# Weight maxima spread over TensorE, and experts' weights loaded in seven parts around tiles in the projections' place

## The chip, the cores and the metric

The kernel runs on one core of a Trainium2 chip. Its time is in microseconds (us) of device time, from the start of the program to its last instruction. A core has TensorE (PE, with its weight loads PEld), VectorE (DVE), ScalarE (ACT), GpSimd (POOL) and SyncE (SP, which here only issues transfers); 16 DMA engines move data. Each engine runs its own instructions in order and waits on semaphores for the others. A wait holds back all that stands behind it on that engine, transfers that it would issue included.

## The reference, cut to what matters

```python
xn = layernorm(x)                                  # x: 4 x 1024 x 512
q, k, v = heads(xn @ Wq.T + bq), ...               # 16 heads of 32
s = q @ k.T / sqrt(32), causal, minus slope * distance
attn = softmax(s) @ v                              # then @ Wo.T + bo
probs = softmax(xn @ gate_w.T)                     # 4096 tokens, 8 experts
topw, sel = top_k(probs, 2); topw /= topw.sum()
g, u = split(xn @ w1[e].T)                         # 2 x 352
ffn = sum over the two chosen e of topw * (silu(g) * u) @ w2[e].T
out = x + attn + ffn
```

All is float32. The kernel writes each operand of a projection as a float16 number and a float16 remainder ("high" and "low"), and forms three of the four products. For that each weight matrix is scaled by a power of two that comes from its largest absolute value.

## The kernel before, in words

`plan()` writes one list of steps. Each engine walks this list and emits its own instructions in that order, so a step's place in the list is its place in every queue it touches. `sync`, `tensor`, `vector`, `scalar` and `gpsimd` hold the instructions of each step. `Once` leaves out waits that are already covered.

**Opening.** SP loads eight tiles of x (128 tokens each), then `bcol`, the gate's weights, four chunks of Wq/Wk/Wv (`w0` to `w3`, 128x1536 each), Wo and the constants `cF`. ACT's queue loads `bv` and `bo` at the very start. A tile is normalized (`bn`, `rsq`, `newton` on POOL, `xn`), split (`xnh` on ACT, `xnl` on POOL), turned on TensorE (`xtp`) and copied out (`xt`). Then come the maxima: `tops` takes each partition's largest value of four chunks on DVE, `gtops` takes the largest over the partitions on POOL (`partition_all_reduce`), `scales` makes the factors, and `wqh` (ACT) and `wql` (DVE) make high and low of each of the four chunks. The projections of batch 0, head group 0 (`qkv_steps(0, 0)`) follow: four `qk` groups of 12 matmuls, each handed on by `qk32` (ACT), `qkh` (DVE) and `qkl` (POOL), and two `v` groups of 48. Woven between them stand `otop`, `gotop`, `woh`, `wol` (the same for Wo), `gwh`, `gwl` and the gate's matmuls of batch 0. `stack` then moves q and k by DMA to where the scores read them.

**Attention.** 512 units (batch, head group, row block, head): `score` on TensorE, `mx` (DVE, adds the distance term and takes the maximum), `exp` (ACT), `tr` (TensorE), `pt` (a copy on ACT or DVE, whichever has less to do), and per 8 units `pv` and `rt`. Later projections, the experts' weight split (`wmax`, `wsh`, `wsl`, `wstore`) and the routing are jobs that give a few steps per unit. The output projection `o` has 12 matmuls for each of 8 row blocks of a batch, `y` (DVE) adds x, `ostore` stores it. The routing leaves the token lists in `tl` (`listr`).

**Experts.** 71 slots of 128 tokens: `gather` (POOL, indirect DMA), `mxt` (DMA transpose, issued by SP), `mgu` (24 matmuls), `msig`, `mglu`, `mah`, `mal` (ACT and DVE), `mat` and `mac` (turned again), `mdn` (9 matmuls, seven slots behind at first), `myo`, and `scatter` (POOL, adds to the output). All weights of the experts lie in SBUF in that phase: 32 pieces, 16 of w1 (704 KB) and 16 of w2 (384 KB). `win` loads them into words 0 to 34816 of `arena` as room comes free there: `win(0)` in place of the projections' weights and of the turned x, `win(1)` in place of the group buffers, `win(2)` (one piece of w1, all of w2) in place of what the last units use. The experts' own tiles (`xg`, `xT`, `ex`, `ac`, `ah`, `aTm`) lie behind the weights and begin after the last unit.

## Time and profile before

| | us |
|---|---|
| median of three runs (1664.79 to 1666.81) | 1664.9 |
| the profiled execution | 1675.45 |
| its span | 1673.6 |
| first `mx` of the attention begins | 83.8 |
| last `o` matmul ends | 1211.3 |
| first `mgu` begins | 1234.0 |
| first `mdn` begins | 1269.0 |

A row of a timeline gives start and length in us, engine, source line, operation, what it writes and reads, how many were merged (x), and in brackets how long the engine had been idle before it and what released it. "issue" stands for a time in which the profile shows no releaser. Mean TensorE clock over the span was 0.96 of full speed.

### The profile page before, as it was taken

What the parts mean: (1) busy time and instruction counts of PE and PEld (TensorE: products, weight loads), DVE (VectorE), ACT (ScalarE), POOL (GpSimd) and SP (SyncE); (2) the same over time, 40 slices, a digit from 0 to 9 for tenths busy, and PEclk for the clock granted to TensorE, in tenths of its full rate; (3) what the DMA queues carried; (4) which work ended last, traced back from release to release, by engine and by line L of the source; (5) the groups of instructions that cost most, each with busy time, mean ns of one, the idle gap of its engine ahead of it and who ended that gap; (6) DMA issues with size and microseconds to landing.
All of it is one profiled execution on the core that took longest, in us unless ns stands there. A gap on an engine that the chain in (4) does not pass through costs nothing.

```text
span 1673.6 us, 35255 instructions
## 1 busy us (share of the span) xinstructions
PE 1473.7 (88%) x12629; PEld 879.6 (53%) x12629; DVE 1027.9 (61%) x2452; ACT 887.7 (53%) x2027; POOL 605.6 (36%) x647
## 2 busy tenths in 40 slices
PE   1599998998998899989799888799949999999995
PEld 1355555555555555655455444455436656565563
DVE  5488778665778767777878846568414333333331
ACT  3277667665777666676766446568312222222221
POOL 3111132121113312112311355351214677777775
PEclk9899999999999999999999889799979999999998
DMA  6053431243243253542214233154286888888884
GB/s 246 18 133 110 133 106 60 72 127 105 92 135 89 74 143 115 151 125 80 91 61 119 83 100 83 49 166 177 93 252 107 133 135 129 131 142 138 129 139 51
DMA packets 173685, 193.42 MB, mean 116 GB/s; under 512 B 89616, under 2 KB 123408, under 8 KB 173392
## 3 DMA queue, kind: packets, MB, share of 16 engines
q1 hardware_dynamic: 143760, 151.22, 33.4%
q0 software_dynamic: 28176, 37.31, 13.5%
q8 instruction: 109, 1.79, 0.4%
q10 hardware_dynamic: 1584, 2.64, 0.4%
q14 instruction: 56, 0.46, 0.1%
HBM read 93.45 MB, written 53.88 MB: 88 GB/s over the span
## 4 chain that ended last, share of the span: by engine, by line
PE 65%; DVE 11%; issue 9%; ACT 5%; SPq 4%; DMA 4%; POOL 2%; another core or an unknown queue 2%; DVEq 0%; ACTq 0%; POOLq 0%
PE S L1074 15%; PE T L1006 11%; PE O L1022 7%; PE S L995 5%; PE M L963 5%; PE S L963 4%; PE O L1105 4%; PE M L1105 4%; SPq L855 3%; DVE arena L1361 3%; PE M L1045 2%; ACT arena L1533 2%; PE S L980 2%; DVE arena L1372 1%
## 5 line engine op out<-in xcount | busy, mean ns | idle before, releaser
L1361 DVE CUSTOM_DVE_ANT_0 arena<-S,cF,nsl 128x1024 f32<-128x1024 f32 (+7 forms) x512 | 413.7, 812 | 69.9 <-PE S L995 60.4
L1006 PE MATMUL T<-cF,arena 128*128 128x128 f32 x2304 | 373.3, 283 | 87.7 <-ACT arena L1543 46.7
L1533 ACT ACTIVATE arena<-arena,mneg 128x1024 f32<-128x1024 f32 (+7 forms) x512 | 395.3, 772 | 44.6 <-DVE mneg L1361 44.1
L1543 ACT ACTIVATE arena<-T 128x512 f32<-128x512 f32 (+3 forms) x543 | 242.2, 459 | 290.2 <-PE T L1006 258.9
L1006 PEld LDWEIGHTS T<-cF,arena 128*128 128x128 f32 x2304 | 270.6, 143 | 193.5 <-issue 53.2
L1074 PE MATMUL S<-arena 128*128 x1704 | 267.7, 314 | 23.0 <-issue 23.0
L1696 POOL DMA_INDIRECT out<-arena,row x142 | 222.3, 1566 | 104.0 <-ACT arena L1595 42.1
L1372 DVE COPY arena<-T 128x512 f32<-128x512 f32 (+3 forms) x289 | 154.0, 535 | 151.5 <-PE T L1006 135.5
L1074 PEld LDWEIGHTS S<-arena 128*128 128x128 f16 x1704 | 167.0, 98 | 120.4 <-issue 23.6
L1022 PE MATMUL O<-arena 128*32 128x128 f32 (+1 forms) x3328 | 214.2, 334 | 8.1 <-DVE arena L1392 6.8
L995 PE MATMUL S<-arena 96*128 96x512 f16 (+3 forms) x768 | 216.1, 336 | 5.5 <-DVE mneg L1361 3.0
L1640 POOL TENSOR_TENSOR arena<-arena 128x512 f16<-128x512 f32 x64 | 74.3, 1161 | 277.1 <-DVE arena L1342 270.0
L1468 DVE COPY arena<-T 128x512 f16<-128x512 f16 x71 | 30.2, 425 | 210.8 <-PE T L1089 186.5
L1650 POOL CAST arena<-arena 128x256 f16<-128x256 f32 x64 | 26.5, 414 | 342.6 <-DVE arena L1392 342.4
L1022 PEld LDWEIGHTS O<-arena 128*32 128x32 f32 x3328 | 67.6, 109 | 132.3 <-issue 116.6
L1580 ACT ACTIVATE arena<-S,sc 128x352 f32<-128x352 f32 x71 | 39.3, 554 | 179.5 <-PE S L1074 166.0
L963 PE MATMUL M<-arena 128*128 128x512 f16 x384 | 99.6, 388 | 14.9 <-DVE arena L1286 14.9
L1657 POOL TENSOR_TENSOR arena<-arena 128x512 f32<-128x512 f32 x32 | 41.0, 1291 | 163.3 <-DMA arena<-in_x 163.3
L1533 ACT ACTIVATION_READ_ACCUMULATOR arena<-arena,mneg 128x1 f32 x512 | 99.9, 195 | 0.0
L963 PE MATMUL S<-arena 128*128 128x512 f16 x384 | 99.8, 388 | 0.0
L1683 POOL DMA_INDIRECT arena<-xn_d,tl x71 | 72.8, 1025 | 60.3 <-DMA arena<-arena 39.3
L1588 ACT ACTIVATE arena<-arena 128x352 f16<-128x352 f32 x71 | 35.2, 496 | 110.4 <-DVE arena L1454 99.5
(169 smaller groups left out, 1808.3 us busy)
## 6 DMA issues: line engine op xcount, KB each, us to landing
arena<-arena SPq DMA_DIRECT2D x192, 128.0 KB
arena<-in_w1T SPq DMA_DIRECT2D x64, 352.0 KB
arena<-in_x SPq DMA_DIRECT2D x64, 256.0 KB, 3.3
w_d<-arena SPq DMA_DIRECT2D x32, 352.0 KB
arena<-w_d SPq DMA_DIRECT2D x16, 704.0 KB, 9.6
arena<-in_w2T SPq DMA_DIRECT2D x32, 256.0 KB
out<-arena SPq DMA_DIRECT2D x32, 256.0 KB, 2.4
xn_d<-arena SPq DMA_DIRECT2D x24, 256.0 KB, 2.0
```

The lines of the kernel that those rows point to most:

```text
L963: tp = pe.matmul(z[:, :], wqkv[:, w_, c, f:f + P], xnT[:, a, c, half * 512:half * 512 + 512], start=(third == 0 and c == 0), stop=(third = ...
L995: tp = pe.matmul(z[:, n0:n1], stk[par][0:96, h, 0, j * P:(j + 1) * P], stk[par][0:96, h, 1, n0:n1], start=True, stop=True)
L1006: tp = pe.transpose(z[:, (c - c0) * P:(c - c0 + 1) * P], ring[u % 4][:, c * P:(c + 1) * P], idf)
L1022: tp = pe.matmul(OB[32 * x:32 * x + 32, f:f + n], V[par][:, kt, x * D:(x + 1) * D], flat[:, x, c * P:c * P + n], start=(kt == 0), stop=(kt ...
L1074: tp = pe.matmul(y[:, i * 512:i * 512 + I], xT[:, s % XDEEP, 4 * a + c, :], weights[:, bass.ds(reg[s] + (w_ * NX * W1N + c * 2 * I + i * I ...
L1105: tp = pe.matmul(z[:, :], aTm[0:n, v, 2 * c + a, :], weights[0:n, bass.ds(r2 + (2 * NX * W1N + w_ * NX * W2N + c * E), E)], start=(k == 0) ...
L1361: dve.tensor_tensor_reduce(ring[r][:, 0:w], SBK[o.bank["score", u]][:, 0:w], rel[:, S - w:S], nsl[:, hh:hh + 1], 3.0e38, ALU.add, ALU.min, ...
L1372: dve.tensor_copy(PT[:, k, h, to_:to_ + gap * (c1_ - c0_ - 1) + 1:gap, :], TB[o.bank["tr", u, i]][:, 0:n].rearrange("p (c n) -> p c n", n= ...
L1533: act.activation(ring[r][:, 0:w], ring[r][:, 0:w], ACT.Exp, bias=mneg[:, m:m + 1], scale=-1.0, accum_out=rs[:, k, c:c + 1]).then_inc(sems[ ...
L1543: act.activation(PT[:, k, h, to_:to_ + gap * (c1 - c0 - 1) + 1:gap, :], TB[o.bank["tr", u, i]][:, 0:n].rearrange("p (c n) -> p c n", n=P), ...
L1640: pool.tensor_tensor(st[:, 2 * qk + 1, lo:hi], t32[:, 0, :], st[:, 2 * qk, lo:hi], ALU.subtract).then_inc(sems["qkl"], 1)
L1696: pool.indirect_dma_start(out=halves, out_offset=bass.IndirectOffsetOnAxis(row[:, part, s:s + 1].bitcast(U32), 0), in_=yo[:, s % YDEEP, c0 ...
```

## The change

1. **Maxima over TensorE.** `gtops` and `gotop` on POOL go. The steps `gmax` and `gtop` take their place twice, for the Q/K/V weights and for Wo: TensorE turns the column of 128 maxima into a row, DVE reduces it and puts it on a small diagonal (`diag`), TensorE multiplies a matrix of ones with that, DVE copies the result to all partitions.
2. **Order of the opening.** `tops` is four steps, the first between the two halves of x. `wqh` and `wql` are cut by head groups: part 0 holds the 128 columns of group 0 of Q, K and V over all four chunks (1536 values per partition), parts 1 to 4 the rest (1152 each). The projections of group 0 wait for part 0 alone.
3. **Later work.** `otop`, the maxima of Wo, `scales 2`, `woh`, `wol` are now a job of the attention's units 0 to 8, `gwh`, `gwl` and batch 0's gate a job from unit 16.
4. **Loads.** `bv` and `bo` move from ACT's queue to SP's, behind `cF` and behind Wo.
5. **SBUF.** The experts' tiles lie at words 0 to 10240, the weights behind them, and room comes free in seven parts. `win(0)` and `win(1)` are fewer pieces, `win(2)` to `win(4)` follow the last score, the last-but-one `pv` and the last `tr`, `win(5)` the last `pv`, `win(6)` the last `o`. The first four gathers and first three transposes are issued during the last units, and slot 0's `mgu` to `mal` stand ahead of the last 16 matmuls of `o`.

```diff
+    def widest(what, part):
+        flush()
+        o.take("M", "gmax", what, part)
+        add("gmax", what, part)
+        yield
+        add("gtop", what, part)
+        o.leave("M", ("gmax", what, part), ("gtop", what, part))
+        yield
...
-    for _ in range(2):
-        next(start)
-    add("scales", 1)
-    add("gwh")
-    add("gwl")
...
-    add("otop")
-    add("gotop")
...
+    for c in range(1, 4):
+        add("wql", 1 + c)
+
+    def first_rest():
+        add("otop")
+        yield
+        for part in range(2):
+            yield from lock()
+            held[0] = False
+            yield from widest("o", part)
+        add("scales", 2)
+        yield
+        add("woh")
+        yield
+        add("wol")
+        yield
...
+            jobs.append((0, 1, 1, 12, first_rest()))
+            jobs.append((16, 1, 1, 32, first_gate()))
...
-    jobs.append((32 * 14 + 28, 1, 1, 32 * 15, win(0)))
-    jobs.append((32 * 15 + 12, 1, 1, 32 * 15 + 14, win(1)))
+    jobs.append((32 * 15 + 2, 1, 1, 32 * 15 + 4, win(0)))
+    jobs.append((32 * 15 + 16, 1, 1, 32 * 15 + 18, win(1)))
+    jobs.append((32 * 15 + 19, 1, 1, 32 * 15 + 26, first_slots()))
+    jobs.append((NU, 1, 1, NU + 2, win(2)))
+    jobs.append((NU + 3, 1, 1, NU + 5, win(3)))
+    jobs.append((NU + 5, 1, 1, NU + 7, win(4)))
...
+    add("win", 5, inc=0)
+    o.turn["S"] = 0
+    up(0)
+    gated(0)
+    now[0] += 2
+    while any(next(job[4], jobs) is None for job in jobs):
+        flush()
+    flush()
+    add("win", 6, inc=0)
...
+                if part == 0:
+                    on.wait_ge(sems["cst"], 16)
+                    on.wait_ge(*(at("tops", 3) if what == "w" else at("otop")))
+                    pe.transpose(z[0:n, 0:P], col(c, n), idf).then_inc(sems["gmax"], 1)
+                else:
+                    on.wait_ge(*at("gtop", what, 0))
+                    pe.matmul(z[:, 0:n], cF[0:n, C_ONE:C_ONE + P], diag[0:n, 0:n], start=True,
+                              stop=True).then_inc(sems["gmax"], 1)
...
+                else:
+                    on.wait_ge(*at("wql", 4))
+                    if u >= 8:
+                        on.wait_ge(*at("wol"))
```

Three places of the order. First DVE, around the first score. `top` is line 1131 (1208 now), `wql` 1286 (1380), `qkh` the CAST of 1342 (1435), `vsb` 1349 (1442), `mx` the ISA rows of 1361 (1454), and M, S0 and S1 are PSUM banks. Before:

```order
L1342 CAST arena<-arena 128x512 [waits s_xtp,s_xnd4,s_xnd5,s_xnd3,s_xnd6,s_qk32]
L1131 TENSOR_REDUCE sc<-arena 128x1 [waits s_w4]
L1342 CAST arena<-arena 128x512 [waits s_qk32] x2
L1125 TENSOR_SCALAR sc<-sc 128x1 [waits s_gotop]
L1126 TENSOR_SCALAR sc<-sc 128x1 [waits s_dstep]
L1127 TENSOR_SCALAR sc<-sc 128x1 [waits s_dstep]
L1128 TENSOR_SCALAR sc<-sc 128x1 [waits s_dstep]
L1318 TENSOR_SCALAR sc<-sc 128x1 [waits s_dstep]
L1322 SCALAR_TENSOR_TENSOR arena<-arena,sc 128x2048 [waits s_woh,s_scales]
L1342 CAST arena<-arena 128x512 [waits s_qk32]
L1349 SCALAR_TENSOR_TENSOR arena<-M,sc,arena 128x512 [waits s_bb,s_v]
L1349 SCALAR_TENSOR_TENSOR arena<-S1,sc,arena 128x512 [waits s_v]
```

and now, from the first `qkh` to the first `mx` and the reduction of Wo behind it:

```order
L1435 CAST arena<-arena 128x512 [waits s_xnd4,s_xtp,s_xnd5,s_xnd3,s_xnd6,s_qk32,s_scales]
L1380 SCALAR_TENSOR_TENSOR arena<-arena,sc 128x3x384 [waits s_wqh]
L1435 CAST arena<-arena 128x512 [waits s_qk32] x3
L1442 SCALAR_TENSOR_TENSOR arena<-M,sc,arena 128x512 [waits s_bb,s_v]
L1442 SCALAR_TENSOR_TENSOR arena<-S1,sc,arena 128x512 [waits s_v]
L1380 SCALAR_TENSOR_TENSOR arena<-arena,sc 128x3x384 [waits s_wqh] x3
L1454 ISA arena,mneg<-S0,cF,nsl 128x1024 [waits s_score]
L1454 ISA mneg 128x1
L1208 TENSOR_REDUCE sc<-arena 128x1 [waits s_w4]
```

The work on Wo has left the chain of the `qkh` and stands among the units, and three `wql` stand between the last `vsb` and the first `mx`.

Second SP, at the end of the attention (`win` is line 911, now 976; `mxt` 917, now 982; `ostore` 870, now 926). Before:

```order
L911 DMA arena<-w1_d 128x2816 [waits s_v,s_wd]
L911 DMA arena<-w1_d 128x2816 x6
L911 DMA arena<-w1_d 128x2816 [waits s_vsb,s_stack13,s_score,s_stack12,s_pv,s_stack11,s_stack10]
L911 DMA arena<-w1_d 128x2816 x7
```

then the stores, and

```order
L870 DMA out<-arena 128x512 [waits s_y] x4
L911 DMA arena<-w1_d 128x2816 [waits s_aT,s_tr,s_rt,s_pv]
L911 DMA arena<-w2_d 128x1536 x16
L870 DMA out<-arena 128x512 [waits s_y] x2
L917 DMA_TRANSPOSE arena<-arena 128x8x128 [waits s_xg0]
```

and now, from the third store of batch 3 on (8 pieces of w1 and three transposes stand ahead of it):

```order
L926 DMA out<-arena 128x512 [waits s_y]
L976 DMA arena<-w1_d 128x2816 [waits s_score]
L976 DMA arena<-w1_d 128x2816 x2
L926 DMA out<-arena 128x512 [waits s_y]
L976 DMA arena<-w1_d 128x2816 [waits s_pv]
L976 DMA arena<-w1_d 128x2816 x2
L976 DMA arena<-w1_d 128x2816 [waits s_tr]
L976 DMA arena<-w1_d 128x2816
L976 DMA arena<-w2_d 128x1536
```

The last eight pieces of w1 are spread over three waits, two of them behind stores that wait for `y`.

Third TensorE at the same place (`o` is line 1045, now 1124; `mgu`'s register load is 1069, now 1146). Before:

```order
L1045 MATMUL M<-arena 128x512 x8
L1045 MATMUL S1<-arena 128x512 [waits s_y,s_aT]
L1045 MATMUL S1<-arena 128x512 x11
L1045 MATMUL M<-arena 128x512 [waits s_y]
L1045 MATMUL M<-arena 128x512 x11
L1069 TENSOR_LOAD off [waits s_win1_0,s_win1_1,s_mxt0,s_win1_2,s_mx,s_route]
```

and now:

```order
L1124 MATMUL M<-arena 128x512 x8
L1124 MATMUL S1<-arena 128x512 [waits s_y,s_aT]
L1124 MATMUL S1<-arena 128x512 x7
L1146 TENSOR_LOAD off [waits s_win1_1,s_win1_2,s_win1_0,s_win1_3,s_route,s_win1_4,s_mxt0,s_mx]
```

with 24 matmuls of `mgu` and the 16 left of `o` behind it. Slot 0 has moved ahead of those 16.

## Rows read from the trace of the kernel before

**Rows 1.** The profile page: the chain that ended last, its share by engine.

```profile
PE 65%; DVE 11%; issue 9%; ACT 5%; SPq 4%; DMA 4%; POOL 2%; another core or an unknown queue 2%; DVEq 0%; ACTq 0%; POOLq 0%
```

**Rows 2.** Busy time by stretch: PE, PEld, DVE, ACT, POOL, clock, DMA share, GB/s.

```profile
92.00:96.00 4.00, 3.86 (x25) 2.28 (x23) 3.73 (x10) 3.86 (x10) 1.16 (x1) 1.00 0.02 4
1215.00:1220.00 5.00, 0.00 (x0) 0.00 (x0) 0.00 (x0) 0.00 (x0) 0.00 (x0) 0.50 1.03 397
1500.00:1600.00 100.00, 100.00 (x661) 60.10 (x660) 35.75 (x81) 27.95 (x51) 74.90 (x53) 1.00 0.86 135
```

**Rows 3.** DMA issues of the first 40 us: KB each, us to landing.

```profile
arena<-in_bv ACTq DMA_DIRECT2D x1, 256.0 KB, 4.3
```

**Rows 4.** Timeline of the opening, from the first x to the first projection.

```profile
18.90 5.38 DVE L1259 TENSOR_SCALAR arena<-arena,mv,nw 128x512 f32<-128x512 f32 x4 [2.37 <-POOL nw L1620]
...
24.61 7.12 DVE L1131 TENSOR_REDUCE sc<-arena 128x1 f32<-128x1536 f32 x4
...
32.93 1.02 ACT L1498 ACTIVATE arena<-S 128x1024 f16<-128x1024 f16 x1 [0.53 <-PE S L932]
37.64 0.38 POOL L1629 PARTITION_ALL_REDUCE sc<-sc  x1 [5.83 <-issue]
...
40.76 7.00 DVE L1286 SCALAR_TENSOR_TENSOR arena<-arena,sc 128x1536 f16<-128x1536 f32 x4 [1.79 <-ACT arena L1504]
...
47.82 5.30 PE L963 MATMUL M<-arena 128*128 128x512 f16 x12 [14.93 <-DVE arena L1286]
...
53.16 0.78 ACT L1523 ACTIVATE arena<-M,bq,cq 128x512 f32<-128x512 f32 x1 [0.19 <-PE M L963]
```

**Rows 5.** Timeline of the opening, on to the first score.

```profile
61.55 0.38 POOL L1632 PARTITION_ALL_REDUCE sc<-sc  x1 [5.89 <-issue]
68.85 1.14 POOL L1640 TENSOR_TENSOR arena<-arena 128x512 f16<-128x512 f32 x1 [6.93 <-issue]
...
74.34 2.35 DVE L1322 SCALAR_TENSOR_TENSOR arena<-arena,sc 128x2048 f16<-128x2048 f32 x1 [2.20 <-ACT arena L1513]
...
75.11 2.84 PE L980 MATMUL S<-arena 128*128 128x128 f16 x48
...
77.83 2.54 PE L946 MATMUL M<-gwh,arena 128*128 128x8 f16 x96
...
78.37 8.36 SPq L855 DMA_DIRECT2D arena<-arena  x12
...
82.72 1.14 PE L995 MATMUL S<-arena 96*128 96x512 f16 x3 [2.35 <-DMA arena<-arena]
...
83.79 1.28 DVE L1361 CUSTOM_DVE_ANT_0 arena<-S,cF,nsl 128x1024 f32<-128x1024 f32 x1 [3.10 <-PE S L995]
```

**Rows 6.** Timeline from the last units into the experts.

```profile
1197.34 9.42 SPq L870 DMA_DIRECT2D out<-arena  x3
...
1205.97 2.76 PE L1045 MATMUL S<-arena 128*128 128x512 f16 x12 [0.42 <-POOL arena L1651]
1206.93 10.54 SPq L911 DMA_DIRECT2D arena<-w_d  x17
...
1220.60 41.43 SPq L917 DMA_TRANSPOSE arena<-arena  x10
1232.53 0.94 POOL L1683 DMA_INDIRECT arena<-xn_d,tl  x1 [20.32 <-DMA arena<-arena]
...
1233.98 9.35 PE L1074 MATMUL S<-arena 128*128 x48 [22.66 <-issue]
...
1243.60 0.53 DVE L1460 TENSOR_TENSOR arena<-arena 128x352 f16<-128x352 f32 x1 [0.56 <-ACT arena L1588]
```

**Rows 7.** The chain that ended last, same place: start, us, what.

```profile
1206.93 4.80 DMA arena<-w_d
...
1245.04 3.75 PE S L1074 x24
...
1269.03 2.01 PE O L1105 x9
```

More of the change, by code:

```diff
@@ L412, in routing, with gather, turn_x, first_slots @@
         yield
+    def gather(s):
+        add("gather", s, sem=f"xg{s % XDEEP}", inc=16)
+    def turn_x(s):
+        add("mxt", s, sem=f"mxt{s % XDEEP}", inc=16)
+    def first_slots():
+        for s in range(XDEEP):
+            gather(s)
+            yield
+        for s in range(XDEEP - 1):
+            turn_x(s)
+        yield
     def win(lo):
@@ L485, in plan, with first_gate @@
                 ln_tile(0, half, i)
+        if half == 0:
+            add("tops", 0)
     load["act"] = load["dve"]
-    add("tops")
-    add("gtops")
+    for c in range(1, 4):
+        add("tops", c)
+    def widest(what, part):
[7 more added lines that the diff above has]
+    for part in range(2):
+        for _ in widest("w", part):
+            pass
     add("scales", 0)
+    add("wqh", 0)
+    add("wql", 0)
     for c in range(4):
-        add("wqh", c)
-        add("wql", c)
+        add("wqh", 1 + c)
+    add("scales", 1)
     start = qkv_steps(0, 0)
-    for _ in range(2):
-        next(start)
-    add("scales", 1)
-    add("gwh")
-    add("gwl")
-    for _ in range(6):
+    for i in range(16):
         next(start)
         flush()
-    add("otop")
-    add("gotop")
-    for _ in range(5):
-        next(start)
-        flush()
-    add("scales", 2)
-    add("woh")
-    add("wol")
+        if i == 5:
+            add("wql", 1)
     for _ in start:
         flush()
-    for _ in ln_gate(0):
-        pass
-    flush()
+    for c in range(1, 4):
+        add("wql", 1 + c)
+    def first_rest():
+        add("otop")
+        yield
+        for part in range(2):
+            yield from lock()
[4 more added lines that the diff above has]
+        add("woh")
+        yield
+        add("wol")
+        yield
+    def first_gate():
+        add("gwh")
+        add("gwl")
+        yield
+        yield from ln_gate(0)
+        yield
     jobs = []
@@ L557, in plan @@
                     next(steps, None)
-    add("win", 2, inc=0)
-    now[0] += 2
-    while any(next(job[4], jobs) is None for job in jobs):
-        flush()
-    flush()
-    s1, m1 = o.tenant["S", 1], o.tenant["M", 1]
-    o.tenant["S", 1] = s1 + m1
-    o.tenant["Y", 0], o.tenant["Y", 1] = o.tenant["O", 0], o.tenant["M", 0]
-    o.turn["T"] = o.turn["S"] = 0
-    def gather(s):
-        add("gather", s, sem=f"xg{s % XDEEP}", inc=16)
-    def turn_x(s):
-        add("mxt", s, sem=f"mxt{s % XDEEP}", inc=16)
     def up(s):
@@ L607, in plan @@
     add("rows")
-    add("experts", inc=0)
-    for s in range(XDEEP):
-        gather(s)
-    for s in range(XDEEP - 1):
-        turn_x(s)
     for s in range(NSLOT + AHEAD):
@@ L810, in build @@
     n_win = {}
-    for k in range(3):
+    for k in range(WINDOWS):
         todo = pieces(LOW[k], LOW[k + 1])
@@ L950, in tensor @@
                     tg.then_inc(sems["gate"], 1)
+            elif kind == "gmax":
+                what, part = key
+                z = MBK[o.bank["gmax", what, part]]
+                c, n = (LW, 3) if what == "w" else (LWO, 1)
+                for s in o.emptied[step]:
+                    on.wait_ge(*at(*s))
+                if part == 0:
[6 more added lines that the diff above has]
+                              stop=True).then_inc(sems["gmax"], 1)
             elif kind == "qk":
@@ L954, in tensor @@
                 if third == 0:
-                    on.wait_ge(*at("wql", 3))
+                    on.wait_ge(*at("wql", 4 if b or g else 0))
                     for i in range(4):
@@ L970, in tensor @@
                 if i == 0:
-                    on.wait_ge(*at("wql", 3))
+                    on.wait_ge(*at("wql", 4 if b or g else 0))
                     for t in range(4):
@@ L1065, in tensor @@
                 on.wait_ge(*at("mxt", s))
-                for k in range(3):
+                on.wait_ge(*at("route", 16))
+                for k in range(WINDOWS):
                     if n_win[1, k]:
@@ L1682, in gpsimd @@
                     on.wait_ge(*at("mxt", s - XDEEP))
+                else:
+                    on.wait_ge(*at("v", B - 1, NG - 1, 1, 3))
+                    on.wait_ge(*at("listr"))
+                    on.wait_ge(sems["z"], 128)
+                    for b in range(B):
+                        for half in range(2):
+                            for i in range(4):
+                                on.wait_ge(*at("xnd", b, half, i))
                 pool.indirect_dma_start(
```

167 lines of the change are left out of this document (90 added, 77 removed).

## Prediction, made before the changed kernel ran

> **What bounds the kernel now.** I read the page's chain first: TensorE holds 65% of it and 9% is "issue", time in which nothing in the profile shows a cause [rows 1]. In the experts' steady part TensorE is busy 100.00 of 100 us, with the DMA engines at 0.86 and POOL at 74.9 of 100 [rows 2]. So what can be won lies where TensorE stands still. The timeline shows two such places. In the opening the first score waits until 82.72 and the first `mx` until 83.79 [rows 5]. Between attention and experts TensorE is idle for 22.66 us before slot 0 [rows 6], and its granted clock falls to 0.50 there, the 1.2 GHz level [rows 2]. The change works on both. The units in between and the slots' loop keep their instructions and, apart from a few steps, their order. I therefore follow two marks: the start of the first `mx`, and the start of the first `mdn` at 1269.03 [rows 7], after which slots come at TensorE's own pace.
>
> **Opening: the first tiles.** `bv` and `bo` leave the front of the transfers. `bv` took 4.3 us to land while x stood behind it [rows 3]. The two are 512 KB, 1.3 us at the 397 GB/s of a full stretch [rows 2]. I take 1.2 us earlier for x and all that follows it; bounds 0 and 1.6. The Trainium skill, "DMA: Bandwidth & Descriptors", section "Issuing engines are not separate DMA queues", would let one expect no gain from a change of queue alone; what I count is the place behind x, not the queue.
>
> **Opening: maxima.** The first `tops` falls into DVE's wait of 2.37 us for `newton` [rows 4] (one reduction is 7.12/4 = 1.78 us), so the second half's `xn` start as before. It costs nothing, and it wins nothing by itself either: reductions end at 31.7, but TensorE and the bank for `gmax` are free only when the last `xt` ends at 33.95 [rows 4]. With the 1.2 us that is 32.75. The second `gmax` and its `gtop` follow at once; the first pair runs beside that `xt`. No row shows the pair; bounds are 0.3 us (two small operations) and the 6.2 us that POOL's reduction took with its wait of 5.83 [rows 4]. Two instructions on engines that have nothing else to do are nearest to the small end: 0.45 us, done at 33.2. POOL was done at 38.02.
>
> From there to the first `wql` were 2.74 us (38.02 to 40.76), and one `wql` takes 7.00/4 = 1.75 [rows 4]. Part 0 is as long as a chunk (1536 values). TensorE's first projection can start at 33.2 + 2.74 + 1.75 + 0.06 = 37.75 instead of 47.82 [rows 4]: 10.1 us earlier, since three `wqh`/`wql` pairs no longer stand ahead of it. The first `qk32` came 5.34 us after TensorE's start (53.16), the time of 12 matmuls at the lower clock level, with `scales 1` done by then; both stay.
>
> **Opening: projections without POOL's reduction.** In the old order POOL idled 5.89 us before Wo's reduction and another 6.93 us after it, and the next `qkl` ended at 69.99 [rows 5]. That holds back every later `qk32`. It goes. TensorE then runs on: 5.30 for the first `qk`, three more at 2.76 (12 matmuls of that shape at full clock [rows 6]), to 51.3; two `v` groups at 2.84 [rows 5], to 57.0. The last `qk` is handed on in about 2.6 us (0.78 on ACT [rows 4], 1.14 on POOL [rows 5], the rest an estimate), so `stack` starts at 53.9. From its start to the first score were 4.35 us (78.37 to 82.72 [rows 5]): score at 58.3. That is not last. DVE has `vsb` (0.8, by the 512 columns of `qk32`) and then three `wql` of 1152 values, 1.31 each from 1.75 x 1152/1536. So the first `mx` starts at 57.0 + 0.8 + 3.9 + 0.3 = 62.0. Before: 83.79. Gain 21.8 us.
>
> At this place a page differs from the row. The Trainium skill, "GPSIMD Engine Reference", section 2.1, says that the first call to a freshly loaded kernel pays about 6 us for loading code. Read as a price paid once, it would leave Wo's reduction cheap, and the gain of this part would be some 12 us less. The row shows 5.89 us again for the second call [rows 5], so the row decides.
>
> **Opening: what is put off.** Wo's and the gate's steps now lie in units 0 to 21. On DVE: `otop` 2048 values (1.78 x 2048/1536 = 2.4), `wol` 2.35 [rows 5], `scales 2` about 1.0 (the 2.74 above less one `wqh`), `gtop`, `gwl`, `lg` about 1.1: 6.9 us. On ACT `woh`, about 2. On TensorE the gate, 2.54 [rows 5]. Behind `otop` on DVE stands the second `mx`; TensorE's `gmax` waits for it with a `qk` and the third score behind. In the old order Wo's and the gate's work lay under waits for POOL and for `stack`; that cover is gone. Is there other cover? In 92 to 96 us DVE is busy 3.73 of 4 us, ACT 3.86, TensorE 3.86 [rows 2]: none. Lower bound 3 us (half of DVE's part found free in later units), upper 11 (DVE's and TensorE's parts in series and 1.6 for the clock). I take 8. Net gain of the opening: 21.8 - 8 = 13.8 us, between 9 and 19.
>
> **Boundary: what slot 0 waits for.** Old: SP issued 17 pieces from 1206.93 in 10.54 us [rows 6], 704 KB of w1 and 16 x 384 KB of w2, and the transposes came behind them. Slot 0's transposed tile was there at 1232.53 (it releases a gather), `mgu` began 1.45 us later, at 1233.98 [rows 6]; that 1.45 is the register load, seen only when the wait is real. New: the first three transposes are done in the units, so the last pieces of w1 decide. Their last two parts stand behind the store that SP issues at 1197.34 [rows 6], so they start at 1197.7; all their other conditions hold by then. The first piece of such a batch lands after 4.80 us [rows 7], each next 704 KB take 1.8 us at 397 GB/s. Five pieces: 1197.7 + 4.8 + 7.2 = 1209.7. TensorE comes to slot 0 at 1205.97 + 8/12 x 2.76 = 1207.8 [rows 6]. With the register load `mgu(0)` starts at 1211.2 and takes 3.75 [rows 7]: 1215.0.
>
> **Boundary: behind slot 0.** The wait sits in TensorE's queue ahead of 16 matmuls of `o` (3.7 us, to 1218.7), and on DVE `mglu(0)` and `mal(0)` stand ahead of `y(3,6)` and `y(3,7)`. From the end of `mgu(0)` to the end of `mal(0)` were about 4.5 us (1239.6 to 1244.13 [rows 6]); so `y(3,6)` ends at about 1220.3. `mgu(1)` needs its bank: start 1221.7 with the load, `mgu(2)` 1226.0. SP stores at 1220.3 and 1221.0, issues `win(6)` (six pieces, 0.62 us each by 10.54/17) to 1225 and only then transposes slot 3, whose data come behind 2.4 MB: about 1230. Slot 3 wants it at 1229.8 plus the load, so 1.2 us are lost. Old `mgu(2)`: 1245.04; from there to the first `mdn` 24.0 us [rows 7]. New first `mdn`: 1226.0 + 24.0 + 1.2 = 1251.2. Gain 17.8 us, between 12 and 22. The w2 pieces have landed by 1229. Gathers and transposes in the units lie in free time of POOL and SP: SP's next store comes later than they end.
>
> **The sum.** 13.8 + 17.8 = 31.6. The profiled execution took 1675.45, so 1643.9 under the same conditions. The median is 10.55 us below that execution; I subtract the same amount: 1633.3, rounded **1633 us**. A difference of 0.2%, some 3 us, is about what a measurement of this kernel can tell from none.
>
> **Rivals.** (a) *The put-off work is hidden.* For it: over the whole attention DVE and ACT have slack. Against: not in 92 to 96 us. It would cost about 1: 1664.9 - 20.8 - 17.8 = 1626. Chance 0.13. (b) *The boundary gives back.* Transposes behind weights are slow: slot 0's was issued at 1220.6 and landed at 1232.53 [rows 6], 12 us. If slot 3's does the same, it is there at 1237, slot 3 starts 7 to 8 us late, and a clock at 0.50 adds 2: 1633 + 9 = 1642. Chance 0.15. (c) *POOL's load is paid once,* as the page has it: 12 us less, 1645. The second wait of 5.89 speaks against it: chance 0.02. (d) *Slower.* The slots' loop leaves its limit by TensorE. DMA share is 0.86, so the transfers of a slot fill 5.0 of its 5.87 us (661 matmuls in 100 us, 39 per slot: 5.9). If the tiles' new place, below the weights, made the transposes or gathers longer so that a slot takes 0.45 us more, 71 slots would cost 32 us and eat all; at 0.6 us the kernel stands at 1676. It decides from transfers that are 27% longer. Nothing in the rows points there: shapes and counts are the same. Chance 0.04.
>
> **How the numbers follow.** The forecast itself has 0.66. Range: opening 9 to 19, boundary 12 to 22, taken together 1624 to 1644; this holds (a) and (b) too and leaves out (d), (c) and the tails. Faster by over 0.2%: 0.66 + 0.13 + 0.15 + 0.02 - 0.01 for a stray = 0.95; within 0.2%: 0.01; slower: 0.04.
>
> **What would show each step.** First projection of TensorE at 37 to 39 us; no wait of some 6 us on POOL before 90 us; `stack` near 54 and first `mx` near 62, with three `wql` right ahead of it. If the first `pv` group comes about 14 us earlier than before and the first `mx` about 22, the put-off work costs 8. At the end the first `mgu` about 3 us after two thirds of `o(3,6)`, all clock rows at 1.00, the first `mdn` about 40 us after `mgu(0)`. The forecast is wrong if `mgu(0)` waits for more than the last w1 pieces, if slot 3's transpose lands later than 1231 less the opening's gain, or if a slot of the steady part takes another time than 5.87 us.

## The result and the profile after

The changed kernel takes 1647.5 us (median of 4 runs, 1643.0 to 1651.9), the kernel before 1665.9 in the same comparison (4 runs, 1664.8 to 1669.8). The ratio is 0.9889, with a 95% interval of 0.9861 to 0.9918. The change gains 18.4 us where I had forecast 31.9, and the time lies above the range of 1624 to 1644. The profiled execution took 1642.96 us, the shortest of its four; that of before, 1675.45, was longer than any of its kernel in this comparison. The two traces are therefore 32.6 us apart (spans 1673.6 and 1641.0), and that looks like my 31.6. It is a coincidence, as will be seen.

The page of the changed kernel, its chain by engine, which answers to [rows 1]: "issue" and DVE have lost two points and one, DMA has one more.

```profile
PE 66%; DVE 10%; issue 7%; DMA 5%; ACT 5%; SPq 4%; POOL 2%; another core or an unknown queue 0%; DVEq 0%; POOLq 0%; ACTq 0%
```

The opening, which answers to [rows 4, 5]. Timeline rows of the changed kernel (start, us, engine and line, operation, in brackets the idle time before it and what ended it):

```profile
30.49 0.42 PE L1025 MATMUL M<-cF,sc 128*3 128x128 f32 x1
...
32.43 0.16 DVE L1370 COPY sc<-S 128x3 f32<-128x3 f32 x1 [0.95 <-PE S L1028]
...
37.23 2.31 PE L1042 MATMUL M<-arena 128*128 128x512 f16 x5 [4.83 <-DVE arena L1380]
...
53.30 7.18 SPq L911 DMA_DIRECT2D arena<-arena  x11
...
56.90 2.74 DVE L1380 SCALAR_TENSOR_TENSOR arena<-arena,sc 128x1152 f16<-128x1152 f32 x2
59.55 1.28 DVE L1454 CUSTOM_DVE_ANT_0 arena<-S,cF,nsl 128x1024 f32<-128x1024 f32 x1
60.76 2.28 DVE L1208 TENSOR_REDUCE sc<-arena 128x1 f32<-128x2048 f32 x1
...
63.19 0.37 PE L1025 MATMUL M<-cF,sc 128*1 128x128 f32 x1 [5.39 <-DVE sc L1208]
```

The maxima's trip over TensorE takes 2.1 us (30.49 to 32.6), the first projection starts at 37.23 and `stack` at 53.30. The first `mx` starts at 59.55, 24.2 us earlier than before [rows 5]. The last row is the one that I did not price: TensorE's part of Wo's maximum waits 5.39 us for `otop`, the row above it, and stands in TensorE's queue ahead of a projection and a score.

The boundary, which answers to [rows 6, 7]. Pieces of the chain that ended last (start, us, what), in order of time:

```profile
1150.07 4.05 DMA out<-arena
1154.14 3.01 DMA arena<-in_x
...
1176.45 12.96 DMA arena<-w_d
1189.41 1.11 issue
1190.52 5.70 PE S L1151 x24
...
1204.27 8.27 DMA arena<-arena
1212.54 1.29 issue
1213.84 5.97 PE S L1151 x24
...
1236.10 2.03 PE O L1182 x9
```

The last piece of w1 lands 12.96 us after its issue, and slot 0's products start at 1190.52 and take 5.70 us instead of 3.75. Slot 3's transpose goes out at 1204.27 and lands 8.27 us later. Its products are slow too. In the steady part nothing has changed: TensorE is busy 100.00 of 100 us at a DMA share of 0.86, as in [rows 2].

```profile
1480.00:1580.00 100.00, 100.00 (x663) 60.28 (x662) 36.90 (x84) 27.25 (x50) 74.69 (x54) 1.00 0.86 135
```

### The profile page after: what moved, and what is told of

The parts are those of the page before. It is cut to its first block, busy times and chain, and to the rows that moved or that the text cites. A ratio compares the mean times of both kernels' runs of the same rounds, so it can differ in the third digit from the quotient of the medians.

```text
span 1641.0 us, 35263 instructions
## 1 busy us (share of the span) xinstructions
PE 1466.7 (89%) x12635; PEld 875.0 (53%) x12635; DVE 1031.2 (63%) x2458; ACT 888.1 (54%) x2029; POOL 603.4 (37%) x645
## 3 DMA queue, kind: packets, MB, share of 16 engines
q0 software_dynamic: 28176, 37.31, 13.9%
## 4 chain that ended last, share of the span: by engine, by line
PE 66%; DVE 10%; issue 7%; DMA 5%; ACT 5%; SPq 4%; POOL 2%; another core or an unknown queue 0%; DVEq 0%; POOLq 0%; ACTq 0%
PE S L1151 15%; PE T L1085 11%; PE O L1101 7%; PE S L1074 5%; PE S L1042 5%; PE M L1042 5%; PE O L1182 4%; PE M L1182 4%; DVE arena L1454 4%; SPq L911 3%; PE M L1124 2%; PE S L1059 2%; ACT arena L1620 2%; ACT arena L1634 1%; DVE arena L1465 1%
## 5 line engine op out<-in xcount | busy, mean ns | idle before, releaser
L1151 PE MATMUL S<-arena 128*128 x1704 | 270.0, 315 | 12.6 <-issue 12.6
L1151 PEld LDWEIGHTS S<-arena 128*128 128x128 f16 x1704 | 167.7, 98 | 111.9 <-issue 13.9
L1761 POOL DMA_INDIRECT arena<-xn_d,tl x71 | 72.0, 1015 | 55.0 <-DMA arena<-arena 32.9
```

What stands on the lines that cost most here:

```text
L1151: tp = pe.matmul(y[:, i * 512:i * 512 + I], xT[:, s % XDEEP, 4 * a + c, :], weights[:, bass.ds(reg[s] + (w_ * NX * W1N + c * 2 * I + i * I ...
```

## Where the two traces part

The instructions of all 512 units can be laid side by side, by the start of each unit's `mx`. At unit 144 the changed kernel is 18.8 us ahead, at unit 400 20.0, at unit 464 29.4, at the first `mdn` 32.9. Nine us of it arise between units 400 and 464, where the experts' lists are written and the change touches nothing. I had both kernels run again (labels f_before and f_after below), and there the stretch is equal in both. Busy time by stretch (PE, PEld, DVE, ACT, POOL, clock, DMA share, GB/s), units 400 to 464 of before, of after, of f_before, of f_after:

```profile
944.30:1115.80 171.50, 144.13 (x1267) 86.01 (x1259) 100.88 (x231) 93.36 (x223) 86.92 (x94) 0.90 0.29 78
```

```profile
924.30:1086.50 162.20, 140.67 (x1267) 83.67 (x1259) 101.59 (x232) 93.32 (x223) 86.61 (x94) 0.91 0.30 82
```

```profile
944.50:1081.70 137.20, 132.30 (x1267) 79.45 (x1259) 101.73 (x231) 92.93 (x224) 87.84 (x94) 0.98 0.35 94
```

```profile
928.10:1065.40 137.30, 132.30 (x1267) 79.51 (x1259) 101.81 (x231) 92.83 (x223) 87.89 (x94) 0.98 0.35 95
```

The same 1267 matmuls take 171.5, 162.2, 137.2 and 137.3 us. The later runs were on other chips, three in all, where the kernel before took 1639 to 1641 us. So this stretch differs by chip: the two profiled executions of the kernel before are 33.8 us apart and their stretches 34.3. That the 9 us between before and after on the first chip are also a matter of the execution is likely, not shown: each kernel has one trace there. In the first trace of before the chain names for the stretch "another core or an unknown queue", which the page of f_before does not have:

```profile
976.22 9.01 another core or an unknown queue
...
1041.21 10.22 another core or an unknown queue
...
1068.63 6.05 another core or an unknown queue
```

These three make 25.3 us. But the first trace of after, whose stretch is 25 us longer than f_after's, has 0% of that entry on its page. So the name does not account for both; what it is, no row tells, and the cause stays open. From here on I compare f_before with f_after and with the variants.

## The experiments

Each variant is the changed kernel with the edit shown, except f_before, which is the kernel before. The kernel before was timed beside every batch (1639.1, 1639.0 and 1640.7 us).

### Both kernels again

> The kernel before, once more, beside the other three on one chip. In its first profiled execution units 400 to 480 took 193.8 us; in four variants on a second chip they took 159 to 185. Theory: that stretch depends on chip and execution, not on the kernel: here it takes 160 to 185 us in this kernel too, and from unit 480 to the first mdn it takes 129 to 131 as before. Rival: the kernel before is slow there by itself (its weights' first window was issued in that stretch): 190 or more.

> The changed kernel once more, on the chip of the other three. Theory: the opening gives 18 to 19 us at unit 64 and the end 4 to 9, wherever it runs; time 22 to 28 us under the kernel before of the same chip. If the first chip's 18.4 us hold everywhere, the end gives nothing. Slot 3's wait of 5 us and the wait of 6 us ahead of slot 0's first products are there again.

f_before: 1641.7 us in its one run, units 400 to 480 in 159.5 us, unit 480 to the first `mdn` in 131.2. f_after: 1619.2 us (4 runs), ratio 0.9874 (0.9836 to 0.9912), 20 to 21 us of gain. The first `mx` is 23.4 us earlier, unit 12 13.9, unit 64 13.5, unit 480 16.3, the first `mdn` 22.7. The rival on the stretch in the middle is out. The end gives 6.4, within my 4 to 9. My 18 to 19 us at unit 64 and my 22 to 28 in all were wrong: in the pair of like executions it is 13.5 at unit 64, the number of the forecast (13.8). Another 2.8 arise between units 64 and 480, 2.3 of them before unit 144, where the change touches nothing; they are in no term of mine. From unit 64 to 144 e_poolmax, f_opool, g_noputoff and the first trace of before take 171.4 us as f_after does, g_best2 takes 173.4 and f_before 173.8, so these 2.3 do not belong to the kernel. The first trace of before had lost 1.4 us more than f_before by unit 4 and 2.5 more between units 28 and 32.

### The end alone

```diff
-    for c in range(1, 4):
+    for c in range(4):
         add("tops", c)
...
-    for part in range(2):
-        for _ in widest("w", part):
-            pass
+    add("gtops")
     add("scales", 0)
...
     for c in range(4):
-        add("wqh", 1 + c)
+        add("wqh", c)
+        add("wql", c)
...
+    add("otop")
+    add("gotop")
...
-            jobs.append((0, 1, 1, 12, first_rest()))
-            jobs.append((16, 1, 1, 32, first_gate()))
```

(`bv` and `bo` are back on ACT's queue too.)

> The changed kernel with the opening of the kernel before (maxima on POOL, all weights split before the first score, nothing put off); arena, windows, early gathers and slot 0 stay as changed. By the prediction's terms the end is worth 17.8 us and the opening 13.8: the time would be about 1648, 18 under the kernel before. Theory after the result: the two traces put about 19 us of the gain into the opening and only 3 to 4 into the end (the rest of their distance is stalls in units 400 to 464 of the one profiled execution of before), so the time is 1662 to 1667, within 4 us of the kernel before. If the middle stalls belong to the kernel before and not to its one execution, this kernel is free of them and comes at 1652 to 1657.

1630.2 us, ratio 0.9942 (0.9921 to 0.9963): the end is worth 9.5 us. Unit 480 to the first `mdn` takes 122.7 us instead of 131.2, 8.5 less. Against f_after's ratio the opening is worth 11. The time missed both of my windows for the end (1648 and 1662 to 1667, which had been meant for a chip of 1666 us; relative to the kernel before, 18 and 0 to 4 less), and lies between them: neither the forecast's 17.8 nor the 3.6 of the first pair of traces. The third guess, 9 to 14 less, has the number but not the reason: it wanted the stalls of the middle to belong to the kernel before, and f_before is free of them.

### Maxima on POOL

```diff
-    for part in range(2):
-        for _ in widest("w", part):
-            pass
+    add("gtops")
...
-            yield from widest("o", part)
+        add("gotop")
```

> The changed kernel with both maxima back on POOL's all-reduce, at the same places in the order; all else as changed. By the prediction's step (scales' input at 33.2 instead of 38.02) the first mx comes 4.8 us later and the time is 1652. Rival: the trip over TensorE saves only what it saves on the way to the scales, 33.2 against POOL's 5.8 us from the last maximum, 3 to 4 us: 1651. Rival: VectorE's later work is what the first score waits for, and the maxima are hidden: 1647 to 1648. Against all three: POOL's second all-reduce and the reload of its library behind it now fall in the slot loop, where they hold up POOL's own work: up to 6 us more, 1656 to 1658.

1615.7 us, ratio 0.9843 (0.9813 to 0.9874); f_after has 0.9874. Taking the trip over TensorE away again costs nothing that can be told from the scatter. The traces say why (start of `mx`, us):

| | unit 0 | unit 12 | unit 64 | unit 480 | first `mdn` |
|---|---|---|---|---|---|
| f_before | 83.22 | 101.13 | 198.88 | 1104.04 | 1235.25 |
| f_after | 59.86 | 87.23 | 185.41 | 1087.73 | 1212.54 |
| e_endonly | 84.06 | 102.41 | 198.84 | 1096.44 | 1219.17 |
| e_poolmax | 65.07 | 87.03 | 186.84 | 1086.43 | 1208.27 |
| f_opool | 59.69 | 81.20 | 178.12 | 1081.42 | 1205.62 |
| g_noputoff | 72.96 | 90.48 | 187.95 | 1089.55 | 1215.30 |

The first `mx` comes 5.2 us later. Of that 1.3 is the execution's and not the maxima's: POOL's last `xnl` ahead of them starts at 29.48 instead of 28.18. The trip itself is worth 3.9, between the forecast's step (4.8) and the first rival (3 to 4). Twelve units on the two kernels are level. No theory had that: the third rival had the time (no loss), but its mechanism, maxima that are hidden before the first score, is out by the same 3.9.

### Only Wo's maximum on POOL

```diff
-        for part in range(2):
-            yield from lock()
-            held[0] = False
-            yield from widest("o", part)
+        add("gotop")
```

> The changed kernel with the projections' maxima left on TensorE and only Wo's maximum, in the slot loop, back on POOL's all-reduce. Theory: in the changed kernel TensorE's own part of Wo's maximum (a transpose that waits 5.4 us for VectorE's 2.28 us of maxima) stands in its queue ahead of a projection and a score, and the 5.5 us that the first mx is earlier against the variant with both on POOL are back at 0.6 by unit 12; off TensorE's queue, unit 0 stays where it is (59.6) and unit 12 starts at about 82 instead of 86.5: 4 to 5 us less. Rival: POOL's library goes in and out there and holds the split of the next projection (3 to 6 us): no gain at unit 12, or a loss of 2. Rival: a gain at unit 12 is given back by unit 64, since VectorE's sum of work up to there is the same.

1614.7 us, ratio 0.9849 (0.9811 to 0.9886), against 1619.2 for f_after beside it. The first `mx` stays, and unit 12 starts at 81.20 instead of 87.23: 6.0 us, a little more than expected; at unit 480 it is 6.3, so nothing is given back by unit 64 or later, and neither rival holds. Against e_poolmax, unit 12 is 5.8 us earlier (1.1 of it by `xnl`, 28.37 against 29.48): with Wo's maximum on POOL the trip of the projections' maxima does pay. TensorE at this place in f_opool, with no 5.39 us wait ahead of projection and score, and POOL:

```profile
59.83 1.89 PE L1040 MATMUL M<-arena 128*128 128x512 f16 x4 [2.11 <-DVE arena L1378]
61.51 1.06 PE L1072 MATMUL S<-arena 96*128 96x512 f16 x2
```

```profile
63.31 0.38 POOL L1712 PARTITION_ALL_REDUCE sc<-sc  x1 [10.19 <-DVE sc L1206]
71.40 1.16 POOL L1720 TENSOR_TENSOR arena<-arena 128x512 f16<-128x512 f32 x1 [7.71 <-DVE arena L1433]
```

POOL starts its reduction 0.1 us after DVE's `otop`: the 5.9 us that [rows 5] shows ahead of it as "issue" lie here in the 10.19 us in which POOL had nothing to do. The Trainium skill, "GPSIMD Engine Reference", section 2.1, has about 6 us for the first call to freshly loaded code. The rows agree in size (5.60 to 5.99 us ahead of a late reduction). That the price comes again with each change of the loaded code fits them too, though no row shows the loading itself; what they show is that it is seen only when POOL is late.

### The put-off work back in its place

```diff
+    for job in (first_rest(), first_gate()):
+        for _ in job:
+            flush()
...
-            jobs.append((0, 1, 1, 12, first_rest()))
-            jobs.append((16, 1, 1, 32, first_gate()))
```

> The changed kernel with the put-off work (Wo's maximum, scales and split, the gate's weights and products) back ahead of the first score; maxima over TensorE and all else as changed. By the prediction's terms the first mx then comes 11 us later and the 8 us that the work costs between the units go: 3 us above the changed kernel. Theory after f_opool: 6 of the 8 to 10 us hang on one waiting instruction in TensorE's queue, which here waits where nothing is queued behind it but the first score: the time is within 2 us of the changed kernel, and 5 to 8 us above f_opool.

1625.6 us, ratio 0.9918 (0.989 to 0.9947). In the table the first `mx` comes 13.1 us later than in f_after, and at unit 12 3.3 us of that are left, at unit 64 2.5, at the first `mdn` 2.8, as the prediction's terms have it (3) and just outside the theory's 2; against f_opool it is 9.7 at the first `mdn`, above the 5 to 8. So the put-off work costs 9.9 us between units 0 and 12, and putting it off with the maximum on TensorE is worth 2 to 3 us by the traces (7 by the medians, with overlapping intervals). With the maximum on POOL it is worth 9 (unit 12: 90.48 against 81.20).

### Transposes in SP's idle time

```diff
     def first_slots():
         for s in range(XDEEP):
             gather(s)
             yield
-        for s in range(XDEEP - 1):
-            turn_x(s)
...
             if i + n < 8:
                 o_load(b, i + n)
+            if b == B - 1 and i == 1:
+                for s in range(XDEEP):
+                    turn_x(s)
```

> The changed kernel with the transposes of slots 0 to 2 moved on SP's queue from ahead of the store of o(3,0) to behind the load for o(3,7), where SP stood idle for 10 us, and slot 3's transpose moved there too, from behind the last window's six pieces. Theory: the three in front held the store, the load for o(3,6), POOL's bias add and the following turn of the arena back (5.6 us lost in units 480 to 511), and slot 3's late transpose cost 5 us of waiting and 2 us of slow clock in mgu(3): 10 to 12 us in all, time 1636 to 1638. Rival, as the prediction had it (SP's queue costs nothing there, only 1.2 us hang on slot 3's transpose): 1646. Rival: what holds the units back is the DMA engines' work, not the place in the queue, and four transposes at 1158 delay the window's pieces by as much: 1645 to 1648.

1608.4 us, ratio 0.9804 (0.9783 to 0.9826), 10.8 us under f_after at an equal time of the kernel before, as expected (10 to 12); both rivals are out. This is the largest single step. Two things went. The first is the loss ahead of unit 511. SP's queue in f_after and in f_best (which has this edit too), from the transposes to the load for o(3,6):

```profile
1122.88 4.45 SPq L982 DMA_TRANSPOSE arena<-arena  x3
1127.37 0.70 SPq L926 DMA_DIRECT2D out<-arena  x1
1131.42 0.34 SPq L921 DMA_DIRECT2D arena<-in_x  x1
```

```profile
1126.18 0.34 SPq L924 DMA_DIRECT2D out<-arena  x1
1128.23 0.33 SPq L919 DMA_DIRECT2D arena<-in_x  x1
```

Against the start of unit 496 (1111.22 and 1111.66) the load goes out after 20.2 us in f_after and after 16.6 in f_best. Over all fourteen profiles the stretch from unit 496 to 511 follows that number: 27.3 us where the load goes at 16.6 (both profiles of before and four variants), 28.3 where it goes at 18.6 to 18.9 (e_poolmax and e_turns4), 31.3 to 31.7 where it goes at 20.2 to 20.5 (all others). Half of the delay is the transposes' place in the queue (store issued 1.6 us later), the other half the store's landing, 4.1 us instead of 2.05; e_turns4 has the slow landing without transposes in front, e_poolmax a fast one (2.5 us) with them, and why stays open. The second is slot 3's wait, 5.1 us in the changed kernel's first trace and 4.5 in f_after, 0.33 here:

```profile
1182.56 3.75 PE L1151 MATMUL S<-arena 128*128 x24 [0.33 <-issue]
```

### Slot 0 behind o(3,7)

```diff
     add("win", 5, inc=0)
     o.turn["S"] = 0
-    up(0)
-    gated(0)
...
     add("win", 6, inc=0)
+    up(0)
+    gated(0)
```

> The changed kernel with slot 0's first products (mgu 0) and what follows them moved from ahead of the last third of o(3,6) to behind all of o(3,7). As the prediction had it, TensorE then does o(3,7) while the weights land and waits for them later, and slot 0 early is worth some 3 us: 1650. Theory after the result: TensorE stands for 6.4 us before mgu(0) with its work of o(3,6) and o(3,7) (about 8 us) queued behind, and the slow clock follows; with that work in front mgu(0) starts about 1192 to 1194 at full clock, ends when it ended before, and mgu(1) follows at once: 4 us gained, and the last window's pieces and slot 3's transpose go out 4 to 5 us earlier too: 1641 to 1644.

1616.5 us, ratio 0.9858 (0.9831 to 0.9884), 2.7 under f_after, with overlapping intervals; the traces say 3.2 at the first `mdn` (66.8 against 70.0 from unit 511). TensorE at the boundary, f_after first, then e_slot0late:

```profile
1166.96 5.97 PE L1151 MATMUL S<-arena 128*128 x24 [5.70 <-issue]
1172.77 1.03 PE L1124 MATMUL S<-arena 128*128 128x512 f16 x4
1173.63 2.75 PE L1124 MATMUL M<-arena 128*128 128x512 f16 x12
1177.38 3.80 PE L1151 MATMUL S<-arena 128*128 x24 [0.99 <-issue]
...
1189.93 6.42 PE L1151 MATMUL S<-arena 128*128 x24 [4.51 <-issue]
```

```profile
1166.91 9.01 PE L1151 MATMUL S<-arena 128*128 x48 [2.20 <-issue]
...
1187.09 6.04 PE L1151 MATMUL S<-arena 128*128 x24 [6.73 <-issue]
```

Slot 0 starts where it started, slot 1 follows at once: from there to slot 2 it is 5.0 us less. Slot 3 gives part of it back, waiting 6.73 us for its transpose instead of 4.51: the transpose goes out 6.7 us earlier, but behind more weights, and lands after 11.5 us instead of 7.6. So slot 0 ahead of the last `o` work was a loss: TensorE stood for weights with work queued behind. That much was as expected. Not as expected are slot 0's products, which start as early as before and are still slow (the two slots take 9.01 us, 7.3 in g_best2 below), and the size lies just under the 3.5 to 6.5 us expected.

### Together

f_best takes three edits (Wo's maximum on POOL, the transposes in SP's idle time, slot 0 behind o(3,7)) and also puts windows 2 and 3 ahead of the stores of o(3,2) and o(3,3); g_nowin leaves that last one out; g_best2 moves the last window.

```diff
-    jobs.append((NU, 1, 1, NU + 2, win(2)))
-    jobs.append((NU + 3, 1, 1, NU + 5, win(3)))
+    jobs.append((NU - 1, 1, 1, NU + 1, win(2)))
+    jobs.append((NU + 2, 1, 1, NU + 4, win(3)))
```

```diff
 (g_best2 against f_best)
-    add("win", 6, inc=0)
...
         if 0 < s and s + XDEEP - 1 < NSLOT:
             turn_x(s + XDEEP - 1)
+        if s == 3:
+            add("win", 6, inc=0)
```

> The changed kernel with four edits together: Wo's maximum on POOL (4 to 5 us); the four first transposes in SP's idle time behind the load for o(3,7) (8 us, as measured by itself); slot 0's first products behind o(3,7) (5 us of mgu(1) against the window's issue); the windows 2 and 3 of the weights ahead of the stores of o(3,2) and o(3,3) on SP's queue instead of behind them (0 to 4 us, as far as the score of the last unit releases the room earlier). Sum 17 to 21 us under the changed kernel. Rival: with all of it the weights' landing is the end's only limit, mgu(0) waits for it as before, and only what the window's issue gains counts: 12 to 14 us.

> The same kernel as f_best, once more, beside its two relatives. In f_best's profile TensorE's granted clock fell to 0.66 in 170:180 and 380:400, where f_opool's did not, and units 48 to 160 took 6.5 us longer with the same instructions. Theory: where the clock falls differs between executions, so this profile shows unit 160 elsewhere than 400.5, and the median stays 31 to 34 us under the kernel before. Rival: it belongs to this kernel's order: unit 160 starts within 1 us of 400.5 again.

> f_best without the earlier windows 2 and 3: three edits (Wo's maximum on POOL, transposes in SP's idle time, slot 0 behind o(3,7)). Windows 2 and 3 go out 2.6 to 4 us later against unit 511. Theory: in f_best TensorE came to mgu(0) with the weights landed and no wait, so that here it waits 2 to 3 us and the time is 2 to 4 us above g_best. Rival: the weights had been there earlier, no difference.

> f_best with the last window's six pieces moved from ahead of slot 4's transpose to behind slot 6's on SP's queue. In f_best TensorE waits 5.19 us for slot 4's transpose (issued behind the six pieces) and its first products then take 5.43 us instead of 3.75. Theory: 6 to 7 us less than g_best. Rival: slots 4 to 7 wait a little each, or the pieces (5 us of transfers) now land after the first mdn wants them: 0 to 3 us less.

| | us | ratio, 95% interval | unit 480 to 511 | unit 511 to mgu(0) | unit 511 to first `mdn` |
|---|---|---|---|---|---|
| forecast, from before's rows | | | 51.0 | 22.0 | 62.0 |
| f_before | 1641.7 | | 51.0 | 44.5 | 80.2 |
| f_after | 1619.2 | 0.9874, 0.9836 to 0.9912 | 54.8 | 24.4 | 70.0 |
| e_slot0late | 1616.5 | 0.9858, 0.9831 to 0.9884 | 54.9 | 24.3 | 66.8 |
| e_turns4 | 1608.4 | 0.9804, 0.9783 to 0.9826 | 51.7 | 24.6 | 63.8 |
| g_nowin | 1606.0 | 0.9808, 0.9777 to 0.984 | 50.8 | 24.8 | 64.1 |
| f_best | 1606.5 | 0.9799, 0.9767 to 0.9831 | 50.8 | 22.0 | 61.0 |
| g_best | 1603.8 | 0.9786, 0.9755 to 0.9817 | 50.8 | 22.1 | 62.1 |
| g_best2 | 1598.3 | 0.9755, 0.9726 to 0.9783 | 50.8 | 22.1 | 55.4 |

f_best missed: 12.6 us under f_after instead of 17 to 21. The rival's 12 to 14 has the number and not the reason: slot 0's products do not wait at all. The profile shows a new late one: with slots 0 to 3 served, slot 4's transpose now stands behind the last window's six pieces on SP. It goes out at 1168.83 and lands 11.85 us later:

```profile
1168.83 11.85 DMA arena<-arena
1180.67 1.47 issue
```

```profile
1182.14 5.43 PE L1149 MATMUL S<-arena 128*128 x24 [5.19 <-issue]
```

The gain of slot 0 behind o(3,7), 3.2 us alone, is therefore not seen in g_nowin next to e_turns4 (64.1 against 63.8). The earlier windows do what was expected: mgu(0) comes 2.7 us earlier, 2 us are left of that at the first `mdn`, and the time differs by 2.2 (2 to 4 expected), with overlapping intervals. The two profiles of f_best's kernel differ, unit 160 at 400.54 and at 398.37 us: more than the 1 us of the rival, though not back at f_opool's 394.00. The second run's median is 37 us under the kernel before (31 to 34 expected). The clock's dips move with the execution, but how much of f_best's loss between units 48 and 160 belongs to its order is not settled.

g_best2 takes the last window out of the transposes' way, and the whole of slots 0 to 7 runs with the clock at 1.00 and waits of 0.81 us at most:

```profile
1155.88 7.33 PE L1150 MATMUL S<-arena 128*128 x48
...
1171.93 3.83 PE L1150 MATMUL S<-arena 128*128 x24 [0.40 <-issue]
...
1185.21 3.75 PE L1150 MATMUL S<-arena 128*128 x24 [0.81 <-issue]
```

```profile
1150.00:1190.00 40.00, 38.07 (x263) 24.21 (x263) 18.14 (x41) 8.04 (x16) 8.18 (x9) 1.00 1.02 301
```

At 1598.3 us it is 5.6 us under g_best beside it (6 to 7 expected) and beats both kernels: 40 us under the kernel before (interval 36 to 45), 19 under the changed one by the ratios. The Trainium skill, "Advanced Engine Details and Errata", section "X-Bar Transpose (TRN2)", has transposes as fast as other transfers. No run here isolates their rate. With no weights queued ahead, f_best's first four land 3.1 to 3.5 us after their issue, where its stores and loads of the same 256 KB take 2.0 and 2.5 to 2.7.

What the move won is the time at which slot 4's transpose is issued, not a faster landing. In g_best2 it goes out at 1159.71, and the gather that it releases starts at 1171.00:

```profile
1159.71 11.23 SPq L981 DMA_TRANSPOSE arena<-arena  x3
...
1171.00 0.96 POOL L1763 DMA_INDIRECT arena<-xn_d,tl  x1 [15.58 <-DMA arena<-arena]
```

That is some 11 us, as in f_best, since nine pieces of w2, issued 3 to 8 us before it, and two stores are still ahead. But counted from unit 511 the issue comes after 25.9 us, in g_best after 31.4.

## Why the prediction was wrong, and where it was right

**The opening's sum was right, 13.8 against 13.5 at unit 64, by two errors that cancel.** That is luck, to 2 us. Most steps held: the maxima done at 32.6 (33.2), first projection at 37.23 (37.75), `stack` at 53.30 (53.9), the first `mx` 23.4 us earlier in the like pair (21.8), with the three `wql` right ahead of it. Of the 1.6 us more, 1.2 are in the first term: I had x and what follows it 1.2 us earlier, and POOL's last `xnl` is 2.4 earlier there (28.18 against 30.59); over the variants with the changed opening it is 1.1 to 2.5. The price of the put-off work was 9.9 us (8). I had counted DVE's and ACT's work for it. What it mostly costs is something else, which I had named in one sentence and not priced: TensorE's `gmax` waiting for `otop` with a projection and a score behind. Without it the work costs 3.6 (f_opool: 23.5 ahead at unit 0, 19.9 at unit 12).

**Maxima over TensorE, as a part, were misjudged.** Of the 4.8 us some 3.9 are real at the first `mx` (e_poolmax), and nothing is left of them at unit 12, because in the changed kernel Wo's maximum takes them back (6.0 us, f_opool). The second 5.89 and the 6.93 us of POOL [rows 5] I took for prices that any use of the reduction pays. They are prices of a POOL that is late.

**The boundary was the step that failed: 17.8 forecast, 6.4 in f_before against f_after, 8.5 in e_endonly.** The table splits the 11.4 us (to 0.4, by which the two traces of before differ there):
- 3.8 between units 480 and 511. The sentence "SP's next store comes later than they end" is false: the store of o(3,0) was due 14.5 us after unit 496 and went out 16.1 after it, and its landing releases the load for o(3,6), POOL's addition and with it TensorE. The row from which I took it free, 1197.34 in [rows 6], is the store of a later `o`.
- 2.4 before mgu(0). From the issue of the first of the five pieces to the landing of the last I had forecast 12.0 us (4.8 + 7.2). In f_after's chain it is 14.7 (the 1.13 us behind it are 0.3 less than my 1.45):

```profile
1151.12 0.43 SPq L976
...
1153.54 12.29 DMA arena<-w_d
1165.83 1.13 issue
```

The mis-sized term is the 4.80 us of the first of the five. It is a landing from a queue with no weights ahead [rows 7]; now three pieces, issued 1145.97 to 1148.81, go ahead, the last of them lands at 1155.87, and the first of the five takes 7.1:

```profile
arena<-w_d SPq DMA_DIRECT2D x1, 704.0 KB, 7.1
```

- 5.6 behind it. Slot 3's transpose, 1.2 us in my sum, cost 4.5 to 5.1 us of waiting and 2.2 to 2.7 of slow clock. This was rival (b) with its mechanism, and it brought 5.6 of its 9 us; I had given it 0.15. The evidence for it stood in my own text: 12 us from issue to landing for slot 0's transpose behind the weights. For the forecast I took 5 for the same thing; it was 8.3 in the first trace of after and 7.6 in f_after.
- The slow clock was left out of the sum altogether: after a wait of 5.70 us slot 0's products take 5.97 us, and the granted clock in that stretch is 0.62, the 1.2 GHz level for most of it. I had forecast all clock rows at 1.00 although my own TensorE was to stand for 3.4 us there.

```profile
1167.00:1173.00 6.00, 6.00 (x26) 3.34 (x27) 0.00 (x0) 0.03 (x1) 0.00 (x0) 0.62 1.03 414
```

**Subtracting 10.55 us** was neither right nor wrong by itself: the profiled execution of before was that much above its median. The stretch in the middle, which no step of mine touched, is the likely place, but no other execution of that chip was traced. It does mean that the distance of the two first traces, 32.6 us, confirms nothing. It is 18.8 at unit 144 (some 2 to 4 of them that execution's), 10.5 from there to unit 480, and 3.6 of the end.

**Rivals.** (a), hidden put-off work, is out: 9.9 us. (c) asked how often POOL's load is paid; it is paid again, but under idle time, and so did not decide as I had it. (d) is out: the first `mdn` to the 71st takes 385.5 us in both first traces.

## What to carry to other kernels

An instruction that is moved forward in a program is also moved ahead of something in its engine's queue: ask for each queue what was due there, and price the wait of all that stands behind, also where the moved work is two tiny matmuls. A transfer that releases the next slot goes ahead of bulk weights on the same queue, and it still takes as long as what was issued before it needs: plan its issue by that, some 11 us here. With each such move, look which transfer is last next. Before a difference between two traces is explained, let each kernel run once more and see which stretches are equal in both.

## What was not expected of the hardware

- The same kernel took 1666 and 1639 to 1641 us on different chips, and by its two traces the difference lies in one stretch, in which POOL writes the experts' lists: 171.5 and 137.2 us for the same 1267 matmuls.
- POOL's 5.9 us ahead of an all-reduce do not show when POOL is idle long enough before its input comes: 0.1 us from `otop`'s end to the reduction in f_opool, after 10.19 us of idle time.
- The store of o(3,0), 256 KB, landed after 2.0, 2.5 or 4.0 to 4.3 us, and the next load hung on it. With the transposes in front, the slow landing cost TensorE 3 us (e_poolmax has 28.3 us, the others 31.3 to 31.7); without them 0.9 (e_turns4, 28.25 against 27.34).
- A transpose of 256 KB landed 3.1 to 3.5 us after its issue with no weights ahead (f_best, slots 0 to 3), and the first one behind weights after 7.6 to 11.9 us.
- After a wait of 4.0 to 6.7 us ahead of slots 0, 3 or 4 the slot's 24 matmuls took 5.1 to 6.4 us instead of 3.75, in every variant that has such a wait.
